# The first gated layer by Strassen's scheme, with the code of the last layer, and x fetched in parts

## The chip, the cores and the metric

The kernel runs on one core of one Trainium2 chip. The metric is the time of one execution on the device in microseconds (us); the median of three runs counts. The engines are TensorE (matmuls), VectorE, ScalarE, GpSimd and SyncE (which only issues DMAs here). In the profile they are called PE, DVE, ACT, POOL and SP; PEld is TensorE's loading of weights.

## The reference

625 tokens of width 1024 in float32. A graph layer comes first (`x + gnn(layernorm(x))`), then a feed-forward block on the layer-normalised rows:

```python
h = x @ lin0_w + lin0_b
h = _swiglu(h, swi1_w1, swi1_b1, swi1_w2, swi1_b2)   # silu(x @ w1 + b1) * (x @ w2 + b2), the first gated layer
h = _moe(h, ...)                                      # top 4 of 8 experts, plus a shared expert
h = h @ lin1_w + lin1_b
h = _swiglu(h, swi2_w1, swi2_b1, swi2_w2, swi2_b2)   # the last layer
```

The result is added to x. All weights are 1024 x 1024, save those of the gate (8 x 1024) and the shared expert (twice as wide).

## The kernel before

Activations are kept transposed: eight chunks of 128 features by 628 columns (625 tokens, padded to two halves of 314, the second with 312 real columns). Precision is kept by splitting each operand in a high and a low part of type fp32r, and by three matmuls per chunk: high x high, weights high x activations low, weights low x activations high (`products`, line 1672). A **unit** is the weights of 128 outputs, [128, 8 chunks, 128]; it is 3 x 8 matmuls for each half of the tokens, 48 in all. Units come from a stream in DRAM: SyncE loads them to four buffers `raw` (line 407 on), ScalarE rounds them to `w_hi` (`split_hi`, 475), GpSimd subtracts to `w_lo` (`split_lo`, 479). All order is written out by hand, with semaphores; each engine works its own program in order.

**lin0** (eight units, line 1878 on) writes `b_hi` and `b_lo`: ScalarE adds the bias (`linear_hi`, 761), VectorE takes the low part (`linear_lo`, 1154). **swi1**, the first gated layer, is 16 units, gate and up in turn (`gated`, 1864): ScalarE takes SiLU of the gate's bank (`gated_pair`, 768), VectorE multiplies (`gated_pair`, 1161), both split the product into `a_hi`, `a_lo`, TensorE turns it to rows (`h_turn`, 1895), and VectorE copies them to `rows` (`h_rows`, 1183). From there they are stored for the gathers of the experts. Then follow the first half of the shared expert (**sha**), eight experts, the other half (**shb**), **lin1** and **swi2**.

**swi2**, the last layer, runs by Strassen's scheme in Winograd's form. Activations and weights are cut in quarters, and seven products of quarters replace eight. A **set** q (0 to 7) is the seven products that give 128 near and 128 far outputs of gate (even q) or up (odd q); a product t is 4 chunks x 3 = 12 matmuls (`quad_product`, 2118). The seven are named by the quarter of the activations, `A11, S2, S3, S1, A12, A22, S4`; set 0 takes them in the order `FIRST_ORDER` (0, 4, 6, 1, 2, 3, 5). Sums of weight quarters are VectorE's: S1, S3, S2 in `sums_first` (1480), S4 in `sum_last` (1489). ScalarE makes each high part (`quad_high`, 869), VectorE each low part (`quad_low`, 1498), save four of set 0, which are GpSimd's (`POOL_QUADS`, 622). VectorE also puts the products together: with u2 (1577), u3 (1583), C22 and u4 (1590, 1591), and the additions of `add_in_place` (1555); ScalarE copies the first product to `p1` (926) and takes SiLU of four quarters (`gate_quad`, 916). TensorE starts set 1 when the second SiLU of set 0 is there, and its product A22 (t = 5) when u3 is. In lin1 the outputs are computed in the order `LIN1_ORDER`, and VectorE forms the sums of activation quarters (`t_sums`, 1504) on the way. Raw weights of set q can be loaded when set q - 2 has been split. The x to be added at the end is fetched in one DMA of 2.5 MB (905), issued as set 0 starts.

Of the kernel before, what the change touches and what calls it, by code (L numbers as in the profile page):

```python
# [10 lines left out]
P = 128  # L11
# [36 lines left out]
def build(nc, x, src, dst, gnn_b, biases, gate, stream, out):  # L48
# [16 lines left out]
    with ctx:  # L65
# [75 lines left out]
        gate_both = act_x[:, 0, 0:KC * GW].rearrange("p (k n) -> p k n", n=GW)  # L141
# [50 lines left out]
        POOL_QUADS = (0, 4, 6, 5)  # L192
        DVE_QUADS = (1, 2, 3)
# [10 lines left out]
        t4_tmp = yr[:, 0:HK * HT].rearrange("p (k n) -> p k n", n=HT)  # L204
        p1, u2 = [yr[:, (HK + n) * HT:(HK + n + 1) * HT] for n in range(2)]
        u4_u3 = yr[:, (HK + 2) * HT:(HK + 4) * HT].rearrange("p (s n) -> p s n", n=HT)
# [10 lines left out]

        def quad_source(q, t):
# [79 lines left out]
        lin0 = Stage("lin0", U_LIN0, gates=False)  # L298
# [4 lines left out]
        lin1_lo = sem("lin1_lo")  # L303
        swi2 = Stage("swi2", U_SWI2, parts=False)
        sha_y = sem("sha_y")
# [93 lines left out]
        LAST_STORES = ((7, 3, NT, 7), (8, 0, 2, 3), (9, 0, 3, 7), (10, 2, NT, 3))  # L399
        out_tiles = out.rearrange("(i p) d -> p i d", p=TT)  # L400
# [6 lines left out]
        def _(sp):  # L407
# [18 lines left out]
            with sp.Fori(1, U_EXP // RING) as g:  # L426
                load_four(g * RING, g * RING)
# [7 lines left out]
            for j, m in enumerate(LIN1_ORDER):  # L435
                sp.wait_ge(hi_split, U_LIN1 + j + 1 - RING)
                sp.wait_ge(lo_split, U_LIN1 + j + 1 - RING)
                sp.dma_start(raw[:, j % RING, :], stream[U_LIN1 + m, :, :]).then_inc(raw_loaded[j % RING], 16)
            for p in range(HK):
                for s, u in enumerate((2 * p, 2 * (p + HK), 2 * p + 1, 2 * (p + HK) + 1)):  # L440
                    q = 2 * p + s // 2
                    if p == 0:
                        sp.wait_ge(hi_split, U_SWI2 - RING + s + 1)
                        sp.wait_ge(lo_split, U_SWI2 - RING + s + 1)
                    elif s % 2 == 0:
                        last_raw = max(RAW_QUADS, key=lambda t: quad_place(q - 2, t))
                        sp.wait_ge(quad_hi, quads_until(q - 2, last_raw))
                        if q == 2:
                            sp.wait_ge(pool_quad_lo, len(POOL_QUADS))
                        else:  # L450
                            sp.wait_ge(dve_quad_lo, lows_until(q - 2, 5))
                        sp.wait_ge(s_sum, 4 * (q - 2) + 4)
                    sp.dma_start(raw[:, s, :], stream[U_SWI2 + u, :, :]).then_inc(raw_loaded[s], 16)
# [6 lines left out]
        def pair_loaded(eng, q):  # L460
            for s in range(2):
                eng.wait_ge(raw_loaded[2 * (q % 2) + s], 16 * (U_SWI2 // RING + q // 2 + 1))

        def arrived(eng, u, off):
            s = off % RING
            if isinstance(u, int):
                eng.wait_ge(raw_loaded[s], 16 * ((u + off) // RING + 1))
                if u + off >= RING:
                    eng.wait_ge(unit_done, u + off - RING + 1)
# [5 lines left out]
        def split_hi(u, off):  # L475
            s = arrived(nc.scalar, u, off)
            nc.scalar.activation(w_hi[:, s, :], raw[:, s, :], ACT.Copy).then_inc(hi_split, 1)  # L477

        def split_lo(u, off):
# [9 lines left out]
            last.then_inc(lo_split, 1)  # L489
# [3 lines left out]
        def _(pool):  # L493
# [36 lines left out]
            for u in range(U_LIN0, U_SHA):  # L530
                split_lo(u // RING * RING, u % RING + 3)
# [89 lines left out]
            pair_loaded(pool, 0)  # L621
            for t in POOL_QUADS:
                n = quad_place(0, t)
                pool.wait_ge(quad_hi, n + 1)
                for c in (slice(0, HW // 2), slice(HW // 2, HW)):
                    last = pool.tensor_tensor(wlo8[:, n, c], quad_source(0, t)[:, c],
                                              whi8[:, n, c].bitcast(f32), ALU.subtract)
                last.then_inc(pool_quad_lo, 1)
# [3 lines left out]
        def _(act):  # L632
# [128 lines left out]
            def linear_hi(st, o_hi, b, pairs):  # L761
                for m in range(KC):
                    split_hi(st.base, m + 3)
                    act.wait_ge(unit_done, st.base + m + 1)
                    act.activation(halves(o_hi[:, m, :]), acc_dense(pairs[m]), ACT.Identity,
                                   bias=bias[:, b, m:m + 1]).then_inc(st.hi, 1)

# [14 lines left out]
            linear_hi(lin0, b_hi, B_LIN0, LIN0_PAIRS)  # L782
            act.wait_ge(gate_loaded, 16)
            act.activation(gate_both[:, :, 0:EXPERTS], gate_cols, ACT.Copy).then_inc(gate_split, 1)
            for m in range(KC):
                gated_pair(swi1, m, a_hi, B_S1A)
# [82 lines left out]
            def quad_high(q, t):  # L869
                n = quad_place(q, t)  # L870
                if n >= 8:
                    act.wait_ge(quad_done, n - 7)
                else:
                    act.wait_ge(unit_done, U_SWI2 - RING + n // 2 + 1)
# [1356 lines left out]
```

## Time and profile before

| | |
|---|---|
| median of three runs | 1587.01 us (1586.23 to 1588.19) |
| the profiled execution's own time | 1587.09 us |
| its span, first to last instruction | 1585.4 us |
| TensorE busy | 1567.0 us (99%), 10892 matmuls |
| VectorE, ScalarE, GpSimd busy | 570.5, 549.0, 799.2 us |
| lin0, from 176.40 | 48.80 us |
| swi1, 225.20 to 341.72 | 116.52 us |
| swi2, from 1470.92 to the end of the span | 114.5 us |

A row of a timeline gives start, duration, engine, line, operation, what it writes and reads, and in brackets how long the engine had stood idle before it and who released it. A matmul's duration includes its latency; two that follow each other overlap, so their distance, not their duration, is their cost.

### The profile page before, as it was taken

How to read it: one execution, taken by the hardware profiler on the slowest of the kernel's cores; microseconds unless marked ns; L12 is line 12 of the kernel's file. 1: busy time of each engine (PE TensorE's matmuls, PEld its weight loads, DVE VectorE, ACT ScalarE, POOL GpSimd, SP SyncE). 2: the span in 40 equal slices, each digit the busy share in tenths (PEclk: the TensorE clock that was granted, in tenths of full speed). 3: DMA queues.
4: the chain of work that ended last, by engine and by line, in shares of the span. 5: the costliest groups of instructions: out<-in, count | busy, mean ns of one | idle time of the engine just before them, and what ended most of it. 6: DMA issues, size and time to landing. Idle time of an engine off the chain costs nothing.

```text
span 1585.4 us, 28313 instructions
## 1 busy us (share of the span) xinstructions
PE 1567.0 (99%) x10892; PEld 1549.6 (98%) x10892; DVE 570.5 (36%) x1045; ACT 549.0 (35%) x824; POOL 799.2 (50%) x673
## 2 busy tenths in 40 slices
PE   9999999999999999999999999999999999999898
PEld 8998999999999999999999999999999999999898
DVE  8665311113420113224241322424221156125787
ACT  6332222222222333343434344344444322224442
POOL 1311233333433666768677686868777576333000
PEclk9999999999999999999999999999999999999999
DMA  4412222232232445546464554646555486221422
GB/s 134 132 41 76 83 67 80 67 108 95 82 98 80 144 142 168 169 126 216 134 191 159 180 170 152 202 143 205 159 175 166 135 221 195 69 78 54 121 88 82
DMA packets 66590, 205.64 MB, mean 130 GB/s; under 512 B 13585, under 2 KB 17335, under 8 KB 66480
## 3 DMA queue, kind: packets, MB, share of 16 engines
q1 hardware_dynamic: 45020, 157.94, 32.8%
q0 software_dynamic: 14976, 32.81, 6.6%
q10 hardware_dynamic: 6484, 13.26, 2.5%
q8 instruction: 88, 1.44, 0.4%
q14 instruction: 22, 0.18, 0.0%
HBM read 185.01 MB, written 18.95 MB: 129 GB/s over the span
## 4 chain that ended last, share of the span: by engine, by line
PE 95%; DVE 2%; ACT 1%; POOL 1%; issue 1%; DMA 0%; SPq 0%; ACTq 0%; POOLq 0%; DVEq 0%
PE acc L1676 88%; PE acc L1656 2%; PE acc L1976 1%; PE acc L1955 1%; POOL w_lo L487 1%; PE acc L1725 0%; DVE yrow L975 0%; ACT act_b L640 0%; DMA rows<-x_dram 0%; DVE yrow L976 0%; POOL gath L539 0%; PE acc L1912 0%; PE acc L2029 0%; PE acc L1667 0%; ACT act_b L645 0%
## 5 line engine op out<-in xcount | busy, mean ns | idle before, releaser
L487 POOL TENSOR_TENSOR w_lo<-raw,w_hi 128x512 fp32r<-128x512 f32 x560 | 718.2, 1308 | 594.0 <-ACT w_hi L477 571.8
L1676 PE MATMUL acc<-act_b,w_hi 128*128 128x314 f32 (+8 forms) x2304 | 512.6, 311 | 0.5 <-ACT gath L918 0.5
L1676 PE MATMUL acc<-act_x,w_hi 128*128 128x344 f32 (+8 forms) x2176 | 479.9, 309 | 4.0 <-POOL w_lo L487 2.6
L1676 PE MATMUL acc<-act_a,w_hi 128*128 128x312 f32 (+1 forms) x1856 | 408.4, 309 | 4.3 <-DVE yrow L1583 4.3
L1676 PEld LDWEIGHTS acc<-act_b,w_hi 128*128 128x128 f32 x2304 | 383.7, 189 | 1.1 <-issue 1.1
L1676 PEld LDWEIGHTS acc<-act_x,w_hi 128*128 128x128 f32 x2176 | 363.7, 188 | 6.0 <-issue 4.8
L1676 PE MATMUL acc<-act_b,w_lo 128*128 128x314 f32 (+8 forms) x1152 | 355.1, 308 | 0.0
L1676 PE MATMUL acc<-act_x,w_lo 128*128 128x312 f32 (+8 forms) x1088 | 336.0, 309 | 0.0
L1676 PEld LDWEIGHTS acc<-act_a,w_hi 128*128 128x128 f32 x1856 | 309.2, 190 | 4.9 <-issue 3.0
L477 ACT ACTIVATE w_hi<-raw 128x1024 fp32r<-128x1024 f32 x280 | 293.8, 1050 | 5.4 <-DVE rows L1189 2.8
L1676 PE MATMUL acc<-act_a,w_lo 128*128 128x312 f32 (+1 forms) x928 | 285.2, 307 | 0.0
L1676 PEld LDWEIGHTS acc<-act_b,w_lo 128*128 128x128 f32 x1152 | 217.6, 189 | 0.0
L1676 PEld LDWEIGHTS acc<-act_x,w_lo 128*128 128x128 f32 x1088 | 204.6, 188 | 0.0
L1676 PEld LDWEIGHTS acc<-act_a,w_lo 128*128 128x128 f32 x928 | 175.4, 189 | 0.0
L1347 DVE TENSOR_TENSOR prod<-acc,silu 128x344 f32<-128x344 f32 x64 | 33.0, 516 | 293.5 <-PE acc L1676 293.5
L1350 DVE TENSOR_TENSOR act_b<-prod,act_b 128x344 fp32r<-128x344 f32 x64 | 98.8, 1543 | 35.7 <-ACT act_b L817 34.0
L817 ACT ACTIVATE act_b<-prod 128x344 fp32r<-128x344 f32 x64 | 31.5, 492 | 188.3 <-DVE prod L1347 177.0
L1339 DVE COPY yrow<-acc 128x256 f32<-128x256 f32 x64 | 27.1, 424 | 172.1 <-PE acc L1976 172.1
L823 ACT ACTIVATE prod<-acc 128x344 f32<-128x344 f32 x64 | 29.3, 457 | 133.4 <-PE acc L1676 133.4
L1329 DVE TENSOR_TENSOR act_x<-acc,act_x 128x344 fp32r<-128x344 f32 x64 | 33.1, 517 | 80.3 <-ACT act_x L797 80.3
L814 ACT ACTIVATE silu<-acc 128x344 f32<-128x344 f32 x64 | 29.2, 456 | 92.9 <-PE acc L1676 92.9
L1656 PE MATMUL acc<-yrow 125*125 125x314 bf16 (+1 forms) x400 | 55.6, 297 | 2.4 <-DVE yrow L976 2.4
(238 smaller groups left out, 1022.8 us busy)
## 6 DMA issues: line engine op xcount, KB each, us to landing
raw<-stream_dram SPq DMA_DIRECT2D x296, 512.0 KB
y_dram<-yrow POOLq DMA_DIRECT2D x16, 512.0 KB
rows<-x_dram ACTq DMA_DIRECT2D x2, 2500.0 KB
y_dram<-yrow POOLq DMA_DIRECT2D x8, 352.0 KB
x_dram<-rows ACTq DMA_DIRECT2D x5, 500.0 KB
h_rows_dram<-rows ACTq DMA_DIRECT2D x1, 2500.0 KB
rows<-x_dram SPq DMA_DIRECT2D x5, 448.0 KB
out_dram<-rows ACTq DMA_DIRECT2D x2, 560.0 KB
```

The lines of the kernel that those rows point to most:

```text
L477: nc.scalar.activation(w_hi[:, s, :], raw[:, s, :], ACT.Copy).then_inc(hi_split, 1)
L487: last = nc.gpsimd.tensor_tensor(w_lo[:, s, c], raw[:, s, c], w_hi[:, s, c].bitcast(f32), ALU.subtract)
L814: act.activation(silu[:, 0:CAP], acc[:, 2 * m % 4, 0:CAP], ACT.Silu).then_inc(exp.silu, 1)
L817: act.activation(g_hi[:, m, :], prod[:, m % 2, 0:CAP], ACT.Copy).then_inc(exp.hi, 1)
L823: act.activation(prod[:, m % 2, 0:CAP], acc[:, m % 4, 0:CAP], ACT.Copy).then_inc(yt_copied, 1)
L1329: dve.tensor_tensor(e_lo[:, m, :], acc[:, TPB + 2 + m % 2, 0:CAP], e_hi[:, m, :].bitcast(f32), ALU.subtract).then_inc(xe_lo, 1)
L1339: dve.tensor_copy(yrow[:, 0:2, m * P:(m + 1) * P], b[:, 0:2 * P].rearrange("p (s d) -> p s d", d=P))
L1347: dve.tensor_tensor(prod[:, m % 2, 0:CAP], acc[:, (2 * m + 1) % 4, 0:CAP], silu[:, 0:CAP], ALU.mult).then_inc(exp.prod, 1)
L1350: dve.tensor_tensor(g_lo[:, m, :], prod[:, m % 2, 0:CAP], g_hi[:, m, :].bitcast(f32), ALU.subtract).then_inc(exp.lo, 1)
L1656: last = pe.matmul(outs[i], oh_dst[0:TT, s, i * TT:i * TT + rows_of(i)], oh_src[0:TT, s, :], start=False, stop=ends)
L1676: ins = pe.matmul(o, w, xs_[h], start=(first and w is hi and xs_ is x_hi), stop=(last and w is lo))
L1955: last = pe.transpose(acc[:, TPB + 2 + m % 2, c0:c0 + cn], grow[0:cn, n, m * P:(m + 1) * P], ident[0:cn, 0:cn])
```

## The change

swi1 takes the scheme of the last layer, and the code of both becomes one. The class `Seven` holds the offsets of the semaphores' counts; `linear_high`, `linear_low`, `quads`, `quad_sums`, `seven` and `load_seven` are the former code of lin1 and swi2 with a parameter `L`. lin0's units come in the order `LIN1_ORDER`.

For swi1, ScalarE and VectorE split the four quarters of outputs as pairs (`out_high`, `out_low`), TensorE turns them (`h_turn`), and ScalarE copies the rows (`h_rows`) that VectorE copied before. Its A22 activations lie in chunks 3 and 7 of `a_hi` and `a_lo`. The first unit of sha is run as two half units, its chunks in the order 0, 4, 1, 5, 2, 6, 7, 3, each waiting for its own output, with the last two turns behind the halves.

For both layers: the low part of the A22 weights of set 0 goes from GpSimd to VectorE; `sums_first` of set 1 stands behind u2 of set 0; `low(1, 0)` behind u3, and so on, as the diff shows; `u4_u3` moves from `yrow` to `gath`. In the last layer x is fetched in four parts of two blocks of 128 columns each (0.64 MB), one at the old place and one after each of the sets 1, 3 and 5.

```diff
-        LIN0_PAIRS = (0, 1, 3, 2, 0, 1, 3, 2)
+        LIN0_PAIRS = (0, 1, 3, 2, 0, 1, 0, 1)
-        POOL_QUADS = (0, 4, 6, 5)
-        DVE_QUADS = (1, 2, 3)
+        POOL_QUADS = (0, 4, 6)
+        DVE_QUADS = (1, 2, 3, 5)
...
+            def raw_free(self, eng, q):
+                last_raw = max(RAW_QUADS, key=lambda t: quad_place(q, t))
+                eng.wait_ge(quad_hi, self.quads + quads_until(q, last_raw))
+                if q == 0:
+                    eng.wait_ge(pool_quad_lo, self.pool_lows + len(POOL_QUADS))
+                eng.wait_ge(dve_quad_lo, self.dve_lows + lows_until(q, 5))
+                eng.wait_ge(s_sum, self.quad_sums + 4 * q + 4)
...
-            act.dma_start(rows[0:TT, :, :], x1_dram.rearrange("(i p) d -> p i d", p=TT)).then_inc(x1_back, 16)
+            def fetch_x1(p):
+                if p >= 1:
+                    act.wait_ge(x1_back, 32 * p)
+                for m in (p, p + HK):
+                    act.dma_start(rows[0:TT, :, m * P:(m + 1) * P], x1_tiles[:, :, m * P:(m + 1) * P]
+                                  ).then_inc(x1_back, 16)
+            fetch_x1(0)
+            def fetch_next(q):
+                if q % 2 == 1 and q + 1 < KC:
+                    fetch_x1(q // 2 + 1)
...
+            def out_high(p, side):
+                m = p + HK * (1 - side)
+                act.wait_ge(swi1.prod, 4 * p + 3 + side)
+                if p == HK - 1:
+                    act.wait_ge(quad_done, quads_until(KC - 1, 5))
+                act.activation(a_hi[:, m, 0:HT + HL], prod[:, 1 - side, 0:HT + HL], ACT.Copy).then_inc(swi1.hi, 1)
+            def h_rows(p, side):
+                m = p + HK * (1 - side)
+                act.wait_ge(h_tp, 2 * p + side + 1)
+                act.activation(rows[0:TT, 0:4, m * P:(m + 1) * P],
+                               acc[0:TT, TPB, :].rearrange("p (i d) -> p i d", d=P), ACT.Copy)
+                act.activation(rows[0:TT, 4, m * P:(m + 1) * P], acc[0:TT, TPB + 1, 0:P],
+                               ACT.Copy).then_inc(h_copied, 1)
+            linear_high(TWO[0])
+            quads(TWO[0], pair_high, far_rows, near_rows)
...
             # VectorE, one set of either layer (quad_sums)
+                    if more and q >= 1:
+                        sums_first(L, q + 1)
+                        quad_low(L, q + 1, 0)
+                    dve.wait_ge(p1_saved, L.p1 + q + 1)
+                    dve.wait_ge(quad_done, L.quads + quads_until(q, 1))
+                    dve.tensor_tensor(u2, acc[:, 1, 0:HT], p1, ALU.add).then_inc(u_done, 1)
+                    if q == 0:
+                        sums_first(L, 1)
+                    elif more:
+                        quad_low(L, q + 1, 1)
+                        sum_last(L, q + 1)
...
+                    dve.tensor_tensor(u4_u3[:, 1, :], acc[:, 3, 0:HT], u2, ALU.add).then_inc(u_done, 1)
+                    if is_gate and p >= 1:
+                        take_out(p - 1, 0)
+                    if q == 0:
+                        quad_low(L, 1, 0)
+                    elif more:
+                        quad_low(L, q + 1, 2)
...
+                    if q == 0:
+                        quad_low(L, 1, 1)
+                        sum_last(L, 1)
+                        quad_low(L, 1, 2)
+                    if more:
+                        quad_low(L, q + 1, 3)
...
             # TensorE
+            seven(TWO[0], h_turn, {})
+            pe.wait_ge(swi1.prod, 4 * (HK - 1) + 2)
+            half_unit(U_SHA, 0, a_hi, a_lo, 0, 0, out_ready, LIN1_ORDER[:6] + (7, 3))
+            h_turn(HK - 1, 0)
+            half_unit(U_SHA, 0, a_hi, a_lo, 1, 1).then_inc(unit_done, 1)
+            h_turn(HK - 1, 1)
```

## Rows read from the trace of the kernel before

**Rows 1.** The page, parts 1 and 2: busy time and share; granted clock in tenths.

```profile
PE 1567.0 (99%) x10892; PEld 1549.6 (98%) x10892; DVE 570.5 (36%) x1045; ACT 549.0 (35%) x824; POOL 799.2 (50%) x673
...
PEclk9999999999999999999999999999999999999999
```

**Rows 2.** The page, part 4: the chain that ended last, by engine.

```profile
PE 95%; DVE 2%; ACT 1%; POOL 1%; issue 1%; DMA 0%; SPq 0%; ACTq 0%; POOLq 0%; DVEq 0%
```

**Rows 3.** Stretch swi1: length; busy PE, PEld, DVE, ACT, POOL; clock; DMA share, GB/s.

```profile
225.20:341.72 116.52, 116.10 (x810) 115.91 (x810) 18.54 (x30) 29.49 (x35) 40.62 (x32) 1.00 0.24 74
```

**Rows 4.** Chain of waits within swi1: start, duration, what.

```profile
253.09 0.55 PE acc L1725 x5
...
268.13 13.91 PE acc L1676 x96
...
339.98 0.88 DVE prod L1170
```

**Rows 5.** Stretches of swi2: sets 2 and 3; sets 4 and 5.

```profile
1507.01:1532.49 25.48, 25.48 (x181) 25.48 (x180) 22.53 (x43) 10.62 (x20) 0.00 (x0) 1.00 0.25 87
1532.49:1557.96 25.47, 25.47 (x180) 25.47 (x180) 22.50 (x43) 10.51 (x20) 0.00 (x0) 1.00 0.34 116
```

**Rows 6.** Timeline of PE in the first sets of swi2.

```profile
1470.92 0.46 PE L1676 MATMUL acc<-act_b,w_hi 128*128 128x314 f32 x2
...
1484.88 0.53 PE L1676 MATMUL acc<-act_a,w_hi 128*128 128x314 f32 x2 [2.82 <-DVE yrow L1583]
...
1487.71 0.86 PE L1676 MATMUL acc<-act_b,w_hi 128*128 128x314 f32 x2 [0.53 <-ACT gath L918]
...
1499.25 0.53 PE L1676 MATMUL acc<-act_a,w_hi 128*128 128x314 f32 x2 [1.52 <-DVE yrow L1583]
...
1502.81 0.46 PE L1676 MATMUL acc<-act_b,w_hi 128*128 128x314 f32 x2
```

**Rows 7.** A split of an output on DVE (timeline); the last product (chain).

```profile
341.65 0.81 DVE L1175 TENSOR_TENSOR act_a<-prod,act_a 128x628 fp32r<-128x628 f32 x1 [0.79 <-ACT act_a L780]
...
1580.73 0.56 DVE prod L1569
```

**Rows 8.** Timeline of DVE in sets 0 and 1 of swi2.

```profile
1479.08 1.24 DVE L1484 TENSOR_TENSOR acc<-raw 128x512 f32<-128x512 f32 x1
...
1481.97 0.68 DVE L1501 TENSOR_TENSOR w_lo<-raw,w_hi 128x512 fp32r<-128x512 f32 x1
1482.57 0.47 DVE L1577 TENSOR_TENSOR yrow<-acc,yrow 128x314 f32<-128x314 f32 x1
1482.96 0.68 DVE L1501 TENSOR_TENSOR w_lo<-acc,w_hi 128x512 fp32r<-128x512 f32 x1
...
1486.53 0.48 DVE L1557 TENSOR_TENSOR acc<-acc,yrow 128x314 f32<-128x314 f32 x1
...
1494.63 0.70 DVE L1484 TENSOR_TENSOR acc<-raw 128x512 f32<-128x512 f32 x1 [4.62 <-DMA raw<-stream_dram]
```

**Rows 9.** Timeline of ACT: the second SiLU of set 0 of swi2.

```profile
1487.04 0.52 ACT L918 ACTIVATE gath<-acc,bias 128x314 f32<-128x314 f32 x1 [0.86 <-DVE acc L1557]
```

**Rows 10.** Timeline of POOL in set 0 of swi2.

```profile
1478.25 2.65 POOL L626 TENSOR_TENSOR w_lo<-raw,w_hi 128x256 fp32r<-128x256 f32 x2 [17.11 <-ACT w_hi L879]
```

**Rows 11.** Stretch with the lower clock, columns as in rows 3.

```profile
1486.25:1489.75 3.50, 2.97 (x13) 2.61 (x12) 3.22 (x7) 2.71 (x6) 0.00 (x0) 0.51 0.45 137
```

**Rows 12.** Timeline of ACT before the first SiLU of swi1.

```profile
227.13 1.28 ACT L775 ACT_TABLE_LOAD   x1
```

**Rows 13.** Timeline of ACT: a copy from PSUM of 500 columns.

```profile
176.01 0.59 ACT L736 ACTIVATE act_a<-acc 128x500 fp32r<-128x500 f32 x1 [5.17 <-PE acc L1835]
```

**Rows 14.** The issue of x (timeline of ACT), and a stretch behind it.

```profile
1475.54 0.49 ACTq L905 DMA_DIRECT2D rows<-x_dram  x1
...
1480.00:1488.00 8.00, 4.65 (x28) 4.06 (x27) 7.72 (x15) 3.08 (x7) 0.90 (x1) 0.90 0.71 187
```

**Rows 15.** Timeline of ACT in set 5 of swi2: four issues of result rows.

```profile
1552.23 2.86 ACTq L909 DMA_DIRECT2D out_dram<-rows  x4
```

More of the change, by code:

```diff
@@ L434, in _ @@
                 load_four(g * RING, g * RING)
[L435 to L453, printed above, removed]
+            load_seven(TWO[1])
             for count, i0, i1, m in LAST_STORES:
@@ L620, in _ @@
                 split_lo(u // RING * RING, u % RING + 3)
[L621 to L628, printed above, removed]
+            quad_lows(TWO[1])
         @block.scalar
@@ new lines, in pair_high, with far_rows, near_rows @@
+            def pair_high(q):
+                if q >= 2 and q % 2 == 0:
+                    out_high(q // 2 - 1, 0)
+                    out_high(q // 2 - 1, 1)
+            def far_rows(q):
+                if q >= 2 and q % 2 == 0:
+                    h_rows(q // 2 - 1, 0)
+            def near_rows(q):
+                if q >= 2 and q % 2 == 0:
+                    h_rows(q // 2 - 1, 1)
+                if q == KC - 1:
+                    for u in range(3):
+                        split_hi(U_SHA, u)
+                    for side in range(2):
+                        out_high(HK - 1, side)
@@ L1678, in products, with unit @@
                 return ins
-            def unit(u, off, x_hi, x_lo, banks, width, ready=None):
+            def unit(u, off, x_hi, x_lo, banks, width, ready=None, count=1):
                 s = off % RING
@@ L1696, in unit, with half_unit @@
                                         w_lo[:, s, k * P:(k + 1) * P], xx[0], xx[1], k == 0, k == KC - 1)
-                last.then_inc(unit_done, 1)
-            def half_unit(u, off, x_hi, x_lo, bank, h, between=None):
+                last.then_inc(unit_done, count)
+            def half_unit(u, off, x_hi, x_lo, bank, h, between=None, order=range(KC)):
                 s = off % RING
@@ L1704, in half_unit @@
                 pe.wait_ge(lo_split, u + off + 1)
-                for k in range(KC):
+                for k in order:
                     if between is not None:
@@ L1864, in gated, with seven @@
+            def seven(L, turn, last_between):
+                for q in range(KC):
+                    for n in range(NQ):
+                        t = FIRST_ORDER[n] if q == 0 else n
+                        quad_product(L, q, t, last_between.get(t) if q == KC - 1 else None)
+                        if q >= 2 and q % 2 == 0 and t in (1, 4):
+                            turn(q // 2 - 1, t // 4)
             def gated(st, x_hi, x_lo, first_ready, after=None, freed=None, begun=False):
@@ L2176, in near_tiles @@
                     last_turn(1, TPB + 3, 0, 3)
[L2178 to L2183 removed]
+            seven(TWO[1], o_turn, {5: far_tiles, 6: near_tiles})
             pe.wait_ge(swi2.prod, 4 * 3 + 4)
```

665 lines of the change are left out of this document (349 added, 316 removed).

## The prediction

> **What bounds the kernel now.** I read the page's parts 1 and 2 first: TensorE is busy 99% of the span, at full clock in all forty slices [rows 1]. Then part 4: 95% of the chain that ended last is TensorE [rows 2]. So time goes only where matmuls go, or where a wait of TensorE appears or vanishes. Next the stretches of the two gated layers. In the first (225.20 to 341.72) TensorE works 116.10 of 116.52 us, while VectorE, ScalarE and GpSimd have 18.5, 29.5 and 40.6 us of work [rows 3]. In its chain 96 matmuls take 13.91 us, 0.145 us each, a turn of rows 0.55, and only at the end something else stands, the last product on VectorE [rows 4]. Last the layer that already runs by seven products, since the changed layer takes its code. Its steady part is clean: 25.5 us for two sets of seven, TensorE busy throughout, VectorE 22.5, ScalarE 10.6 [rows 5]. Its first two sets are not: set 0 starts at 1470.92, TensorE has waits that end at 1484.88, 1487.71 (where set 1 starts) and 1499.25, and set 2 starts at 1502.81 [rows 6]. That is 31.89 us for 2 x 84 matmuls that need 24.4: 7.5 us lost.
>
> **Part 1, matmuls.** Removed: 16 units of 48 = 768. Added: 8 sets x 7 products x 4 chunks x 3 = 672. 96 fewer, 13.9 us off the engine that bounds [rows 4]. The eight turns stay (4.4 us), and the two half units that open the next layer are the 48 matmuls of the unit they replace.
>
> **Part 2, the end of the first layer.** Before, 116.52 less 768 x 0.145 and 4.4 leaves 0.7 us, the wait for the last product. After, the next layer starts at once and takes the two last outputs only in its chunks 7 and 3. From the last quarter product VectorE adds (0.48), multiplies (0.56) and splits two outputs (0.81 each) [rows 7, 8]: 2.7 us; TensorE has 21 matmuls = 3.0 us before it needs the second. Hidden, so I take 0.7 off; bounds 0 and 0.7.
>
> **Part 3, set 0 of the first layer.** This stall is new there, and I size it by following VectorE's queue in the last layer. Before, it ran from 1479.08 without a gap: S1, S3, S2, low(1,0), u2, low(1,1), S4, u3, low(1,2), C22, u4, low(1,3), then at 1486.53 the addition that releases the SiLU at 1487.04, which releases set 1 [rows 8, 9]. (low(q,t) is the low part of weights of product t in set q; u and C are sums of products.) After, the queue reads: low(0,5) (taken over from GpSimd), u2, S1, S3, S2, u3, low(1,0), C22, u4, low(1,1), S4, low(1,2), low(1,3), the same addition. Successive starts give 0.60 for an operation of 512 columns and 0.39 for one of 314. S1, S3 and S2 took 2.89 together, not 1.80, with GpSimd at work from 1478.25 to 1480.90; S1 alone took 1.24 there and 0.70 at 1494.63, with GpSimd idle [rows 8, 10]. GpSimd has left its last piece to VectorE, so I use 0.60. Sum: 9 x 0.60 + 4 x 0.39 = 6.96, where it was 7.45. Set 1 starts 0.5 us earlier, 16.3 us after set 0 instead of 16.8. u3 ends some 2.3 us earlier, which shortens the wait at 1484.88, but what is late next is the SiLU, so this time comes back as a wait of about 2.9 us before set 1. Stall of set 0 in either layer: 16.3 - 12.2 = 4.1 us; the first layer has the same queue and takes it whole. Bounds: 3.7 (its data come 0.4 earlier, as the linear layer's last unit is no longer pressed by anything) and 5.2 (S1 and S3 slow again).
>
> The clock belongs to this. From 1486.25 to 1489.75 it was granted at 0.51, the lower of its two levels, 1.2 GHz instead of 2.4, after TensorE had stood for 2.8 us and run again for 1.4; of 2.97 us of matmuls half was lost, 1.46 [rows 6, 11]. The new stall is of the same kind and I take 1.3 us in each layer; bounds 0 and 1.7. The Trainium skill (TensorE: Matmul & The Clock Gate, What's actually happening) says that the monitor is free-running and does not start with the kernel; by that the same stall may be caught or missed, and the sum would be this one or 2.6 us less. One fall in one trace can't decide it.
>
> ScalarE meets one thing here that the last layer lacks: its first SiLU loads a table, 1.28 us [rows 12]. Behind its splits of S2, S3 and S1 (about 1483.5 on the last layer's clock) it would end at 1484.8; the first SiLU is then done at 1485.3, and the one that matters can start at 1486.6. Cost 0, with 1.3 us of cover. The Trainium skill (ScalarE: Activation LUTs, What ACT_TABLE_LOAD costs) adds a drain of about 1380 ns to the load; by that the estimate is a cost of 0.1 us. The row can't show it, since ScalarE had nothing to do behind the load.
>
> **Part 4, sets 1 to 7 of the first layer.** The work of the last layer, except that on VectorE two splits of outputs (0.81) stand for the sums of result rows, and ScalarE gets two output splits (0.7) and two copies of rows (0.59 for 500 columns and some 0.3 for the rest) on top: 10.6 + 3.2 = 13.8 us in 25.5 [rows 5, 7, 13]. Cost 0: in the steady part neither engine held TensorE up. If that cover is gone, about 1 us per even set, 3 us.
>
> First layer: -13.9 - 0.7 + 4.1 + 1.3 = **-9.2 us**.
>
> **Part 5, the last layer.** Its set 0 gains 0.5. In set 1 VectorE stood 4.62 us for the weights of set 2, until 1494.63, and was so late with u3 that TensorE waited until 1499.25 [rows 6, 8]. This 1 MB could be issued when GpSimd finished at 1480.9 and shared the engines with the 2.5 MB of x issued at 1475.54; 187 GB/s moved [rows 14]. After, the first part of x has 0.64 MB. At the same 187 GB/s from 1476 on, 1.7 MB are there by 1485; VectorE asks for them at 1489.1 (the addition, two more, three splits). Then u3 of set 1 is ready by 1494 and TensorE wants it at 1497: the wait goes, 1.7 us with its restart, and nothing is late next. The clock's loss stays (1.3 for 1.5). Before 7.5 lost, after 4.1 + 1.3 = 5.4: **-2.1 us**; bounds 0 and -3.5. The later parts are issued by ScalarE between sets. Four issues of this kind took its queue 2.86 us at 1552.23, and TensorE ran on [rows 5, 15]. Two cost half; in set 5 six together end about 1.4 us later, and the copy behind them is due when u2 is, some 1.5 us after its data. Cost 0; uncovered 0.7 per part, 2 us.
>
> Moved scratch space, shared counters, the gate's columns and the other bank pairs of the linear layer cost nothing: bank pair 0 is asked for again a unit (7 us) after ScalarE could read it, and its two reads take 1.6. On SyncE's queue the same loads stand in the same order; those of set 2 wait for VectorE's low(0,5) at 1479.7, not for GpSimd's at 1480.9.
>
> **Sum.** -9.2 - 2.1 = -11.3 us. The profiled execution took 1587.09 (its span 1585.40), the median of the runs is 1587.01, 0.1 lower: forecast **1575.8 us**.
>
> **Rivals.**
> *Clock not caught*: neither stall brings it down. For: the waits are 0.5 us shorter in sum. Against: the longest one stays as long [rows 6, 11]. 1575.8 - 2.6 = 1573.2. Chance 0.12.
> *ScalarE's added work is late*: the output splits stand ahead of the quarter splits in its order. Against: it is busy 54% of the set. 1575.8 + 3 = 1578.8. Chance 0.10.
> *The parts come too slowly*: pieces of 512 bytes instead of 4 KB hold the weights up all the same, and the 1.7 us of set 1 don't go. For: each part has as many pieces as the whole. Against: 4 us of slack. 1577.5. Chance 0.08.
> *Slower*: GpSimd's reads. While it works an operation of VectorE with two SBUF inputs takes 0.54 us more [rows 8, 10]. VectorE has 11.3 us of work in a set of 12.7 and becomes the bound once GpSimd meets more than two of its eight such operations in a set. All eight: 4.3 more, 2.9 over, over seven sets 20 us, so 1596. Against: GpSimd's program has nothing to do between set 0 and the end of set 7, where VectorE has little left. Chance 0.03.
> Forecast 0.67.
>
> **How the numbers follow.** The first three rivals and the bounds of parts 3 and 5 give 1573.0 to 1579.5; the slower one lies outside. What a measurement can tell from no change is about 0.2%, 3.2 us, so everything below 1583.8 is faster. Faster 0.95, same 0.02 (several losses at once), slower 0.03.
>
> **What would show it.** 96 matmuls fewer. In the first layer 106 us from the start of set 0 to the next layer's first matmul, with two turns behind it. In each gated layer one wait of about 2.9 us before set 1, and one of 0.7 before the product on A22; full clock from set 2 on; in the last layer no wait of VectorE for weights in set 1. Wrong if TensorE waits in sets 2 to 7 of the first layer, if the linear layer before it grows, or if the experts' stretch changes.

## The result, and the profile after

The changed kernel took 1579.13 us (median of five runs, 1576.38 to 1581.06) where the kernel before took 1587.01 (1586.23 to 1588.93): ratio 0.9946, 95% interval 0.9935 to 0.9956. (The ratios of this document are not quotients of the two medians beside them; by the ratio the gain is 8.6 us.) So it is faster by 7.9 us; forecast were 11.2, and the time lies inside the range of 1573.0 to 1579.5, near its slow end. The profiled execution took 1576.51 us (span 1574.8), 10.6 less than that of before: the forecast's 11.3 nearly holds there. That is in part luck: in this execution the clock did not fall in the last layer, and this hid about as much as a wait that the forecast did not have.

The page after: busy time, granted clock, and the chain by engine. 96 matmuls fewer and 12.7 us less of TensorE's time than in [rows 1]; more of the chain is off TensorE than the 5% of [rows 2].

```profile
PE 1554.3 (99%) x10796; PEld 1536.2 (98%) x10796; DVE 658.4 (42%) x1207; ACT 584.2 (37%) x913; POOL 764.6 (49%) x645
...
PEclk9999999999999999999999999999999999999999
...
PE 93%; DVE 3%; POOL 1%; issue 1%; ACT 1%; ACTq 0%; DVEq 0%; POOLq 0%
```

The stretch of the first gated layer, two of its steady sets, set 1 of the last layer and two steady sets there (columns as in [rows 3]):

```profile
225.22:331.56 106.34, 102.81 (x704) 102.13 (x703) 86.99 (x157) 54.95 (x102) 7.05 (x6) 0.98 0.27 89
276.93:302.40 25.47, 25.47 (x181) 25.47 (x180) 22.40 (x41) 13.16 (x26) 0.00 (x0) 1.00 0.24 83
1478.65:1494.40 15.75, 15.75 (x109) 15.75 (x110) 13.59 (x26) 7.70 (x15) 0.00 (x0) 1.00 0.29 90
1507.00:1532.48 25.48, 25.48 (x180) 25.48 (x180) 22.51 (x43) 10.64 (x21) 0.00 (x0) 1.00 0.34 108
```

The first layer takes 106.3 us from set 0 to the next layer's first matmul (forecast 106), and its steady sets are the last layer's: 25.47 us with ScalarE at 13.2 (forecast 13.8). All that it loses is in its first 20 us. TensorE's timeline, set 0 and the start of set 1 of that layer (the bracket is the wait before the row, and who ended it):

```profile
232.19 0.52 PE L1773 MATMUL acc<-act_x,w_hi 128*128 128x314 f32 x2 [0.29 <-DVE act_b L1291]
...
236.89 0.52 PE L1773 MATMUL acc<-act_a,w_hi 128*128 128x314 f32 x2 [0.58 <-DVE gath L1351]
...
241.52 0.53 PE L1773 MATMUL acc<-act_b,w_hi 128*128 128x314 f32 x2 [2.66 <-ACT gath L849]
241.89 0.36 PE L1773 MATMUL acc<-act_b,w_lo 128*128 128x314 f32 x1
242.04 0.73 PE L1773 MATMUL acc<-act_b,w_hi 128*128 128x314 f32 x2
...
245.59 0.30 PE L1773 MATMUL acc<-act_x,w_lo 128*128 128x314 f32 x1
```

Set 0 starts at 225.22 and set 1 at 241.52: 16.3 us, as forecast, with the long wait where it was forecast. From 242.0 to about 245.5 a matmul takes 0.46 to 0.47 instead of 0.31. The stretch within it (columns as in [rows 3]), and the chain over set 1:

```profile
242.00:245.20 3.20, 3.20 (x15) 3.20 (x14) 3.07 (x6) 2.71 (x6) 0.00 (x0) 0.50 0.31 61
```

```profile
240.85 0.53 ACT gath L849
241.38 0.14 issue
241.52 17.40 PE acc L1773 x108
258.92 0.55 PE acc L1822 x5
```

108 matmuls at 0.145 need 15.7 and took 17.4 in this chain; TensorE's timeline has the turn at 258.76, 17.2 us after the start of set 1. The lower level (1.2 GHz) cost 1.5 us by the timeline. ScalarE ahead of it, with the table load of the first layer:

```profile
237.98 1.28 ACT L849 ACT_TABLE_LOAD   x1
239.27 0.52 ACT L849 ACTIVATE gath<-acc,bias 128x312 f32<-128x312 f32 x1
240.85 0.52 ACT L849 ACTIVATE gath<-acc,bias 128x314 f32<-128x314 f32 x1 [1.06 <-DVE acc L1322]
```

The load was hidden: behind it ScalarE still had 1.06 us to wait for the addition. The last layer, TensorE's timeline:

```profile
1469.32 0.52 PE L1773 MATMUL acc<-act_x,w_hi 128*128 128x314 f32 x2 [0.29 <-DVE act_b L1291]
...
1474.02 0.53 PE L1773 MATMUL acc<-act_a,w_hi 128*128 128x314 f32 x2 [0.58 <-DVE gath L1351]
...
1478.65 0.53 PE L1773 MATMUL acc<-act_b,w_hi 128*128 128x314 f32 x2 [2.65 <-ACT gath L849]
...
1552.31 0.78 PE L1822 MATMUL acc<-ident,prod 128*125 128x128 f32 x5 [1.04 <-DVE rows L1711]
```

The wait of 1.52 us in set 1 [rows 6] is gone, and in this execution the clock stayed up. But at 1552.31, in set 6, there is a wait that the kernel before didn't have. The chain that leads to it goes back to ScalarE's queue (ACTq are the instructions on it that issue DMAs), here as its timeline at the end of set 5, and the stores' first two pieces in the chain:

```profile
1540.31 0.63 ACT L816 ACTIVATE w_hi<-gath 128x512 fp32r<-128x512 f32 x1 [1.11 <-PE acc L1773]
1540.32 1.79 ACTq L1007 DMA_DIRECT2D rows<-x_dram  x2
1542.15 5.75 ACTq L1014 DMA_DIRECT2D out_dram<-rows  x4
1548.03 0.63 ACT L816 ACTIVATE w_hi<-raw 128x512 fp32r<-128x512 f32 x1 [7.08 <-PE acc L1773]
```

```profile
1542.15 2.96 ACTq L1014
...
1545.14 1.64 ACTq L1014
```

Issuing six DMAs held ScalarE for 7.6 us; the four stores alone had taken 2.86 [rows 15], and behind the part of x the same four take 5.75, most of it the first two. (The last row's bracket names PE, but in the chain the issues stand right before that split.) ScalarE's next split is late, so VectorE's low part and sums are, and among them the addition to `rows` that frees the bank of the next turn.

### The profile page after: what moved, and what is told of

Read it like the earlier page. It is cut to its first block, busy times and chain, and to the rows that moved or that the text cites. A ratio compares the mean times of both kernels' runs of the same rounds, so it can differ in the third digit from the quotient of the medians.

```text
span 1574.8 us, 28380 instructions
## 1 busy us (share of the span) xinstructions
PE 1554.3 (99%) x10796; PEld 1536.2 (98%) x10796; DVE 658.4 (42%) x1207; ACT 584.2 (37%) x913; POOL 764.6 (49%) x645
## 4 chain that ended last, share of the span: by engine, by line
PE 93%; DVE 3%; POOL 1%; issue 1%; ACT 1%; ACTq 0%; DVEq 0%; POOLq 0%
PE acc L1773 86%; PE acc L1753 2%; PE acc L2144 1%; PE acc L2123 1%; POOL w_lo L512 1%; DVE yrow L1056 1%; DVE yrow L1055 1%; PE acc L1822 0%; ACTq L1014 0%; DVE w_lo L1278 0%; POOL gath L577 0%; PE acc L2080 0%; PE acc L2197 0%; PE acc L1738 0%; PE acc L1764 0%
## 5 line engine op out<-in xcount | busy, mean ns | idle before, releaser
L512 POOL TENSOR_TENSOR w_lo<-raw,w_hi 128x512 fp32r<-128x512 f32 x528 | 680.9, 1316 | 609.8 <-ACT w_hi L502 587.6
L1773 PE MATMUL acc<-act_x,w_hi 128*128 128x312 f32 (+8 forms) x2304 | 508.5, 309 | 4.3 <-POOL w_lo L512 2.6
L1773 PE MATMUL acc<-act_b,w_hi 128*128 128x312 f32 (+8 forms) x2048 | 456.9, 312 | 5.3 <-ACT gath L849 5.3
L1773 PE MATMUL acc<-act_a,w_hi 128*128 128x314 f32 (+1 forms) x1920 | 422.6, 309 | 1.2 <-DVE gath L1351 1.2
L1773 PEld LDWEIGHTS acc<-act_x,w_hi 128*128 128x128 f32 x2304 | 385.6, 188 | 6.6 <-issue 4.8
L1773 PE MATMUL acc<-act_x,w_lo 128*128 128x312 f32 (+8 forms) x1152 | 355.8, 309 | 0.0
L1773 PEld LDWEIGHTS acc<-act_b,w_hi 128*128 128x128 f32 x2048 | 340.9, 189 | 5.8 <-issue 5.8
L1773 PE MATMUL acc<-act_b,w_lo 128*128 128x314 f32 (+8 forms) x1024 | 316.0, 309 | 0.0
L1773 PE MATMUL acc<-act_a,w_lo 128*128 128x314 f32 (+1 forms) x960 | 294.8, 307 | 0.0
L1773 PEld LDWEIGHTS acc<-act_b,w_lo 128*128 128x128 f32 x1024 | 193.5, 189 | 0.0
## 6 DMA issues: line engine op xcount, KB each, us to landing
rows<-x_dram ACTq DMA_DIRECT2D x8, 312.5 KB
```

The lines of the kernel that those rows point to most:

```text
L512: last = nc.gpsimd.tensor_tensor(w_lo[:, s, c], raw[:, s, c], w_hi[:, s, c].bitcast(f32), ALU.subtract)
L1773: ins = pe.matmul(o, w, xs_[h], start=(first and w is hi and xs_ is x_hi), stop=(last and w is lo))
```

## Stages of the executions

Each ratio is against runs of the kernel before on the same chip (medians 1587.0, 1588.5, 1587.7 and 1587.4 in the four series), and the text goes by it rather than by the difference of medians. "Start" is when TensorE begins its last turn of rows ahead of lin0, "middle" from there to the end of the 0.3 us wait in set 0 of the last layer (7 us into it), then "sets 0, 1" from there to the first turn (early in set 2), and "sets 2 to 7" from that to the end of the last wait of TensorE; each is a difference of starts in TensorE's timeline of the one profiled execution.

| kernel | median us | ratio to before, 95% | start | middle | sets 0, 1 | sets 2 to 7 |
|---|---|---|---|---|---|---|
| before | 1587.01 | 1 | 175.38 | 1302.52 | 28.41 | 75.02 |
| changed | 1579.13 | 0.9946 (0.9935 to 0.9956) | 175.57 | 1293.75 | 25.08 | 76.31 |
| changed, again | 1579.34 | 0.9943 (0.9930 to 0.9956) | 177.67 | 1293.76 | 26.58 | 76.29 |
| x whole | 1576.52 | 0.9928 (0.9915 to 0.9941) | 175.57 | 1293.55 | 27.79 | 75.03 |
| parts, stores by SyncE | 1576.71 | 0.9925 (0.9911 to 0.9938) | 177.58 | 1292.91 | 25.07 | 75.02 |
| last layer alone | 1588.45 | 0.9999 (0.9990 to 1.0007) | 177.60 | 1303.64 | 25.07 | 77.33 |
| last layer, order alone | 1586.40 | 0.9998 (0.9989 to 1.0007) | 176.00 | 1302.97 | 25.63 | 75.52 |
| last layer, parts alone | 1588.50 | 1.0007 (0.9997 to 1.0017) | 174.94 | 1302.67 | 25.56 | 77.47 |
| early addition | 1571.83 | 0.9900 (0.9884 to 0.9917) | 177.54 | 1290.84 | 23.00 | 76.23 |
| free bank | 1571.97 | 0.9903 (0.9886 to 0.9919) | 175.06 | 1290.63 | 23.54 | 76.38 |
| both | 1571.87 | 0.9905 (0.9888 to 0.9921) | 175.39 | 1289.53 | 23.00 | 76.68 |
| both, x whole | 1574.74 | 0.9924 (0.9910 to 0.9937) | 175.85 | 1292.19 | 27.18 | 75.02 |
| all edits | 1570.54 | 0.9897 (0.9881 to 0.9914) | 175.06 | 1290.78 | 23.01 | 75.03 |

## Experiments

**The changed kernel again**, for a second profile. Two theories on what the median lacks stood against each other: A, ScalarE's issues block it for a time that varies; B, the clock behind the stall of the last layer.

> The changed kernel once more, beside the kernels of this call. Theory A (ScalarE's DMA issues in the last layer block it for a time that varies): the profile again shows the four stores at the end of set 5 as a block of 5 us or more and TensorE waiting about 1 us in set 6, and where the block is longer the wait and the whole time are longer. Theory B (the clock after the stall of set 0 of the last layer): the profile has the same block, but a time near 1578 to 1580 goes with a granted clock near 0.5 for 3 us behind that stall, and one near 1576.5 with a clock of 1.00 there. Both: ratio to the kernel before 0.9935 to 0.9956, as it was.

The stores took 5.53 us and the wait was again 1.04, so in these two profiles A's cost is steady: it costs, but nothing shows that it spreads the runs. The clock did fall in the last layer this time (TensorE's stretch from 1481, columns busy, matmuls, clock, DMA):

```profile
1481.00:1485.00 4.00, 4.00 (x20) 0.64 0.36 88
```

Sets 0 and 1 took 26.58 for 25.08: 1.5 us. Another 2.1 us were lost before anything of the change runs, in "start"; that is treated in the last section.

**x fetched whole, at the old place.**

```diff
-            fetch_x1(0)
+            act.dma_start(rows[0:TT, :, :], x1_tiles).then_inc(x1_back, 16)
...
-                if q % 2 == 1 and q + 1 < KC:
-                    fetch_x1(q // 2 + 1)
```

> x fetched as one DMA at the old place, the rest as in the changed kernel. Theory A: with no fetch of a part at the end of set 5 the stores on ScalarE's queue take about 2.9 us again in place of 7.5, TensorE's wait of 1.0 us in set 6 is gone, and the spread of the runs is again near 2.7 us. Against it stands what the one DMA costs in set 1: if the weights of set 1 come late again, TensorE waits up to 1.5 us there. Sum between 1.0 us faster and 0.5 us slower than the changed kernel (median 1578.1 to 1579.6). Theory B: median as the changed kernel's within 0.5 us but for that wait, and the spread stays at 4 to 5 us. The rival of the forecast that the order of VectorE's work alone removed the weights' wait: no wait in set 1.

The block shrank and the wait in set 6 went, 76.3 to 75.03 us. ScalarE at the end of set 5:

```profile
1542.83 2.95 ACTq L1007 DMA_DIRECT2D out_dram<-rows  x4
```

The median is 2.8 us lower than the changed kernel's beside it. That is more than the 1.3 the trace shows and more than was expected; the intervals overlap. The one transfer did hold up the weights, by 2.85 us for VectorE, and TensorE did not wait, but it ran at the lower level itself for about 6 us (2.7 us lost) and so needed the products later. VectorE in set 1, and TensorE's stretch from 1481:

```profile
1483.59 0.70 DVE L1252 TENSOR_TENSOR acc<-raw 128x512 f32<-128x512 f32 x1 [2.85 <-DMA raw<-stream_dram]
```

```profile
1481.00:1485.00 4.00, 4.00 (x18) 0.56 0.97 250
```

The spread of the runs stayed at 4.9 us, which is against A. It is not proof of B: the 17 runs of the kernel before in this series spread over 5.2 us, where five had spread over 2.7 at first.

**Parts and stores issued by SyncE.**

```diff
                         sp.dma_start(raw[:, s, :], stream[L.swi + u, :, :]).then_inc(raw_loaded[s], 16)
+                    if L.n == 1:
+                        fetch_x1(p)
...
             load_seven(TWO[1])
+            sp.wait_ge(o_rows, 4)
+            store(0, NT, 0, 2 * P)
+            store(0, NT, HK * P, (HK + 2) * P)
```

> The parts of x and the output stores of sets 5 and 7 issued by SyncE, none by ScalarE in the sets of the last layer. Theory A: no block on ScalarE, no wait of TensorE in set 6, 1.0 us off the profiled time and the spread back near 2.7 us; median about 1577.5. Theory B: the 1.0 us goes too, but the spread of 4 to 5 us stays, since the clock is what varies. A loss of 1 us or more in sets 2 to 7 would show that the loads on SyncE's queue, which now stand behind parts and their waits, are late.

No block, sets 2 to 7 back at 75.02, weights in time, 1576.71. The spread was 6.1 us. So the parts cost nothing by themselves, and neither do the stores on ScalarE's queue (75.03 with x whole); what costs is both on ScalarE's queue. Parts by SyncE with the stores left to ScalarE were not run.

**Only the last layer's share, and its two halves.** The kernel before with the last layer's order and parts; with the order alone; with the parts alone.

```diff
-POOL_QUADS = (0, 4, 6, 5)
-DVE_QUADS = (1, 2, 3)
+POOL_QUADS = (0, 4, 6)
+DVE_QUADS = (1, 2, 3, 5)
...
+            fetch_x1(0)
...
+                if q % 2 == 1 and q + 1 < KC:
+                    fetch_x1(q // 2 + 1)
```

> The kernel before with the last layer's new order and the parts of x, its first layer left with eight products. Forecast's sum: 2.1 us faster than the kernel before (ratio 0.9987), so the first layer is worth 9.2. By the trace of the changed kernel: the last layer there gave 3.6 with the clock kept, or 2.1 with it lost, less 1.0 for the new wait in set 6, so 1.1 to 2.6 us faster (ratio 0.9984 to 0.9993). Theory A: its spread is wide, like the changed kernel's. Theory B: also wide, if the clock of the last layer is what varies; a narrow spread would put the variation in the first layer, where the stall of set 0 is new.

> The kernel before with only the new order of the last layer (A22's low part on VectorE, the sums and low parts of set 1 moved), x still fetched as one DMA. My prediction took 0.5 us from set 0 and 1.7 from the weights of set 1. If the order alone brings the weights in time (they are free earlier, since SyncE's wait is met sooner), the wait of 1.5 us in set 1 is gone and from the start of set 0 to the first turn is 32.1 us as in the changed kernel with the clock kept, 2.1 to 3.3 us less than before: ratio 0.998 to 0.9985. If the parts of x are needed for it, the wait in set 1 stays at 1 us or more, and VectorE waits for the weights' DMA until some 21 us after the start of set 0. In both, ScalarE's four stores at the end of set 5 take 2.9 us, and no wait of TensorE in set 6.

> The kernel before with x fetched in parts and nothing else of the change. If the parts make the weights of set 1 come in time, the wait of 1.5 us in set 1 goes; set 0 stays as it was, with its waits of 2.8 and 0.5 us. Against it ScalarE's queue: the part and the four stores at the end of set 5 hold ScalarE 7 to 9 us, and TensorE waits 1.0 to 1.9 us in set 6 and the set before, as measured in the kernel with the last layer's change alone. Sum: -1.7 + 1.3 to 2.3, so within 0.6 us of the kernel before on either side: same.

The last layer's change is worth nothing that can be measured: 0.9999, where 0.9987 was forecast. The first layer's is the difference, 0.9999 - 0.9943 = 0.0056 of 1588.5, 8.9 us (forecast 9.2), give or take 2.4 by the two intervals. The stretches agree: 116.52 less 106.34, less the two turns of 0.55 that now stand behind the next layer's start, is 9.1. Where the 2.1 us went, the trace says: sets 0 and 1 gained 3.3, of which 1.3 is the clock (kept in this execution, lost in that of before) and 2.0 the order and the parts, and sets 2 to 7 gave 2.3 back, 1.85 of it in two waits in set 6. TensorE's timeline of the kernel with the last layer's change alone:

```profile
1562.08 0.53 PE L1697 MATMUL acc<-act_b,w_hi 128*128 128x314 f32 x2 [0.65 <-ACT yrow L934]
...
1565.26 0.78 PE L1746 MATMUL acc<-ident,prod 128*125 128x128 f32 x5 [1.20 <-DVE rows L1557]
```

The halves: with the order alone VectorE's wait for the weights fell from 4.62 to 2.32 us and TensorE's from 1.52 to 0.31, between the two outcomes expected:

```profile
1492.92 0.70 DVE L1483 TENSOR_TENSOR acc<-raw 128x512 f32<-128x512 f32 x1 [2.32 <-DMA raw<-stream_dram]
```

```profile
1497.55 0.53 PE L1684 MATMUL acc<-act_a,w_hi 128*128 128x314 f32 x2 [0.31 <-DVE yrow L1585]
```

With the parts alone both are gone, but sets 2 to 7 take 77.47. So either half removes most of the wait that the forecast counted once for both. By their intervals neither half can be told from no change. In this kernel VectorE got the weights 4.62 us after the start of set 1 with the clock kept; with x whole in the changed kernel it was 5.15 us, so at full clock TensorE would have waited some 0.8 us there (an estimate from these rows).

**The stall before set 1.** What else is to be had there? TensorE waits 2.65 us for the SiLU of C11, and that for an addition standing behind four operations of VectorE whose results are due later. First edit:

```diff
                     if q == 0:
+                        add_in_place(4, p1, HT)
                         quad_low(L, 1, 1)
...
-                    add_in_place(0 if q else 4, p1, HT)
+                    if q >= 1:
+                        add_in_place(0, p1, HT)
```

> The changed kernel with the addition for C11 of set 0 moved ahead of the low part of A22, of S4 and of two more low parts on VectorE, in both gated layers. Theory (the stall of 2.65 us before set 1 is VectorE's order, since SiLU of C11 waits for the addition behind four other operations): in the last layer the addition starts 2.4 us earlier, the wait before set 1 falls from 2.65 us to 0.1 to 0.5, and TensorE's clock stays at 1.00 behind it; in the first layer ScalarE loads its table (1.28 us) ahead of the first SiLU, so the wait there falls only to about 1.3. Sum: 2.3 and 1.3 us of waits, and 1.2 to 1.5 us of clock in the first layer if it is kept: 3.5 to 5 us under the changed kernel, near 1575. Rival (the low parts behind it become late, since set 1 needs them in its first 3 us): a wait of 0.5 us or more before A22's or S4's product of set 1, and under 2 us gained.

The wait fell to 0.24 us in the last layer and 1.49 in the first, where the table load now stands in the way. TensorE's timeline, and ScalarE's and VectorE's ahead of the first of these waits:

```profile
242.32 0.53 PE L1775 MATMUL acc<-act_b,w_hi 128*128 128x314 f32 x2 [1.49 <-DVE w_lo L1278]
...
1475.30 0.53 PE L1775 MATMUL acc<-act_b,w_hi 128*128 128x314 f32 x2 [0.24 <-DVE w_lo L1278]
```

```profile
239.95 1.28 ACT L849 ACT_TABLE_LOAD   x1
241.24 0.93 ACT L849 ACTIVATE gath<-acc,bias 128x312 f32<-128x312 f32 x2
```

```profile
241.50 0.68 DVE L1278 TENSOR_TENSOR w_lo<-gath,w_hi 128x512 fp32r<-128x512 f32 x1
```

The bracket names VectorE's low part, which ended at 242.18. That one is low(1,2), and the first product of set 1 doesn't wait for it; what the code makes it wait for is the second of the two SiLUs, which ended at 242.17.

From 242.32 to the turn it takes 15.71 us: the clock was kept. The median is 1571.83, ratio 0.9900 for 0.9943, 6.8 us by the ratios; 3.5 to 5 were expected. The traces show 2.7 of it in the first layer and 2.1 (against the changed kernel with the clock kept) to 3.6 (lost) in the last. The rest fits the clock as recorded for every run, not only the profiled one: its mean over the execution was 0.996 to 0.998 in the five runs of the changed kernel beside the first experiments, 0.9972 on average, and 1.000 in all four here. 0.0028 of 1575 us is 4.4 us of matmul time, an estimate from figures rounded to 0.001; with the 3.6 us of shorter waits that is 8.0, for 6.8 by the ratios and 7.5 by the medians.

Second edit. In set 0 C11 has a bank of its own, so bank 0 is free once product 0 is copied out; TensorE's wait for two SiLUs there names a bank that it doesn't write.

```diff
-                if t == 0:
+                if t == 0 and q == 1:
+                    pe.wait_ge(p1_saved, L.p1 + 1)
+                elif t == 0:
...
+                elif t == 3 and q == 1:
+                    pe.wait_ge(u_done, L.u + 3)
```

> The changed kernel with one wait less for a reason: in set 0 the sum C11 stands in a bank of its own, so the first product of set 1 waits for the copy of product 0 out of bank 0 instead of the SiLU of C11; the order of the other engines is as it was. Theory (the stall is only a wait for a bank that is free anyway): the wait of 2.65 us before set 1 is gone in both layers, and a shorter one comes later in set 1, where the third product needs bank 3, whose SiLU ends 2 us behind that of C11: product 2 is due 3.1 us into set 1, so a wait of about 1.2 us. Gain 1.4 us per layer, and since neither wait is above 1.3 us the clock is kept: 1.2 to 1.5 us more per layer where it fell. Sum 3 to 5.5 us under the changed kernel. Rival (the total idle time decides the clock, not the longest wait): gain of 2.5 to 3 only.

As expected, 2.65 became a later wait of 1.1 in either layer (1571.97, ratio 0.9903, 6.4 us by the ratios where 3 to 5.5 were expected):

```profile
242.98 0.54 PE L1773 MATMUL acc<-act_b,w_hi 128*128 128x314 f32 x2 [1.14 <-ACT gath L849]
...
1476.98 0.52 PE L1773 MATMUL acc<-act_b,w_hi 128*128 128x314 f32 x2 [1.10 <-ACT gath L849]
```

and the clock was 1.00 behind both. In the first layer, set 0 lost the clock in all four profiles with the 2.65 us wait in one piece and keeps it here with waits of 0.3, 0.6 and 1.1. That does not decide against the rival by which the sum of idle time counts, since that sum also fell, from 3.5 to 2.0; that both longest wait and sum are smaller is all that is shown. Both edits together:

> Both edits, the early addition and the free bank. Theory: no wait over 0.3 us before or in set 1 of the last layer; in the first layer the table load of 1.28 us still stands before the SiLUs, and it now delays only the third product, by up to 1 us. Sum against the changed kernel: 2.65 + 2.65 of waits less 0.3 and 1.0, so 4.0, and the clock of 1.3 to 2.7 us where it fell: near 1573.5 to 1575. If the clock still falls in the first layer with waits this short, the idle time of set 0 (0.29 and 0.58) is what it reacts to, and the sum is 4 us.

0.3, 0.6 and 0.4 us of waits are left in either layer, and sets 0 and 1 take 23.00. The median (1571.87) is no lower than with one edit, so of what the second edit adds the runs can show nothing. The traces have a little: from the 0.3 us wait of the first layer to its turn 22.99 us, against 23.86 with the early addition alone and 23.53 with the free bank alone, and in the last layer 23.00 against 23.00 and 23.54. That is 0.9 to 1.1 us in all, less than the spread of these runs (3.0 us).

**Both edits, x whole.** This takes away the stall behind which one transfer looked harmless.

> The changed kernel with the early addition and the free bank, and x fetched as one DMA at the old place. With x whole the weights of set 1 landed 2.9 us after VectorE asked for them, and TensorE did not wait, but its clock was low there for 6 us and it was late by 2.7 us. Here set 0 has no stall and the clock should be kept, so the cover is gone: if the parts are worth something, TensorE waits 1 to 2.5 us in set 1 of the last layer for a product whose low part is late, and the sum is -1.2 (no block in set 6) + 1 to 2.5 against the kernel with both edits and the parts by ScalarE (1571.9): 1571.7 to 1573. If one transfer does no harm after all: 1570.5 to 1571, as with SyncE's issue.

TensorE waited 2.81 us in set 1 and lost the clock on top: sets 0 and 1 took 27.18, 4.2 us more than 23.00. TensorE, VectorE and ScalarE in set 1:

```profile
1484.66 0.86 PE L1764 MATMUL acc<-act_b,w_hi 128*128 128x314 f32 x2 [2.81 <-ACT yrow L862]
```

```profile
1483.54 0.70 DVE L1252 TENSOR_TENSOR acc<-raw 128x512 f32<-128x512 f32 x1 [4.29 <-DMA raw<-stream_dram]
```

```profile
1483.57 0.63 ACT L816 ACTIVATE w_hi<-raw 128x512 fp32r<-128x512 f32 x1 [5.14 <-DMA raw<-stream_dram]
1484.10 0.41 ACT L862 ACTIVATE yrow<-acc 128x314 f32<-128x314 f32 x1
```

The way it came was not the expected one, a late low part of VectorE's. What TensorE waited for is ScalarE's copy of the first product (`yrow`, L862), and in ScalarE's program that copy stands behind the split of the next set's raw weights, which waited 5.14 us for the DMA. An order in which the copy comes first was not run.

The median is 1574.74 for 1571.87, more than forecast; the two were measured on different chips, and their ratios, 0.9924 and 0.9905, have intervals that overlap. The traces show it more plainly: 4.2 us lost in sets 0 and 1, 1.7 gained in sets 2 to 7. So the parts are worth about 2.5 us once set 0 is quick, with the stores' queue left as it is.

**All edits**: both, the parts and stores by SyncE, and the SiLU table loaded ahead of the layer, by this line of ScalarE's before lin0:

```diff
+            act.activation(ones[0:TT, 1:2], ones[0:TT, 0:1], ACT.Silu)
```

> Both edits, the SiLU table loaded ahead of the layer by a SiLU of one element a row, and the parts of x and the stores of sets 5 and 7 issued by SyncE. Theory: besides the gains of the two edits, the wait of 1.0 us in set 6 is gone (1.2 us as measured between the changed kernel and the one with SyncE's issue) and 1 us at the table load. Median 1571 to 1573; against the kernel before a ratio near 0.990. Rival: the kernel's opening, 0 or 2.1 us later in all kernels so far, and the clock elsewhere hide part of it: the median above 1573.

1570.54 us, ratio 0.9897: 7 to 9 us below the changed kernel (by ratios or by medians), a little under its expected range. Sets 0 and 1 at 23.01 and sets 2 to 7 at 75.03 are the best seen in one kernel; over the kernels with one edit its lead of 1.3 us is within the intervals. The earlier table load gave nothing here: from the 0.3 us wait of the first layer to its turn it takes 23.01 us with it and 22.99 without, since with the free bank no SiLU holds TensorE.

## Why the prediction was right, and where it was not

*Matmuls (-13.9) and the end of the layer (-0.7)*: 96 fewer; the next layer begins at 331.56 without a wait. *Set 0 (+4.1)*: 16.30 us in the first layer, 16.31 in the last, for 16.3. Following VectorE's queue by successive starts was exact (from low(0,5) at 233.37 to the addition at 240.33, 6.96 for 6.96), and the prediction that u3's earlier end comes back as a wait before set 1 too (2.65; forecast 2.9). *Table, splits and copies (0)*: hidden.

*Clock (+1.3 in each layer)*: right in kind, near in size for the first layer, and no constant in the last. In the first layer TensorE's timeline has from the start of set 1 to the first turn 17.24, 16.99, 17.27 and 16.97 us in the four profiles that have the stall, for 15.71 without: 1.3 to 1.6 lost each time. In the last layer the same span took 15.75, 17.25, 18.47, 15.75 and 15.74 in five profiles: nothing, 1.5, 2.7, nothing, nothing (a sixth, with the order alone, 15.99 without its wait of 0.31); 2.7 lies beyond the bound of 1.7. The old order of set 0 shows the same: with waits of 2.8 us and 0.5 to 0.8 before set 1 the kernel before lost 1.3 us, and the one with the parts alone nothing (15.75). The rule weighed in part 3 (the Trainium skill, TensorE: Matmul & The Clock Gate, What's actually happening: a free-running monitor) fits the last layer, where one stall of 2.65 us was caught in some executions and missed in others, but in the first layer it was caught every time. Why the two layers differ no run shows.

*First layer*: 8.9 us measured by difference and 9.1 by the stretches, 9.2 forecast.

*Last layer (-2.1)*: 0.2 us measured, between 1.6 gained and 1.1 lost. The step that failed is part 5's "in set 5 six together end about 1.4 us later" and its "Cost 0". Six issues held ScalarE 7.6 us, not 4.3; the sets after it took 1.3 us longer in the changed kernel and 2.3 longer with the last layer alone. I had one row (four stores, 2.86 us) and assumed that issues add up. Four stores cost 2.9 alone and 5.5 to 6.9 right behind a part's two issues. The forecast named the uncovered cost itself (0.7 per part, 2 us) and gave it no rival. With 1.3 us put there it is 1577.1, and with the clock as measured in the four profiles with the stall (from 1.3 less to 1.7 more) 1575.8 to 1578.8, for a median of 1579.1. What is left is smaller than what "start" alone varies by, 2.1 us. (The sum is off by 0.1: 1587.0 - 11.3 is 1575.7.)

*Rivals*: ScalarE's added work in the first layer was not late (TensorE has no wait there behind set 1); the parts did not come too slowly. GpSimd had no occasion to slow VectorE: it has no operation from 215.4 to 322.9, VectorE's nine wide operations of set 0 ran at 0.60 us each, and beside GpSimd's six in set 7 TensorE did not wait. "Clock not caught" happened, for one of the two layers, in the profiled execution.

What stays open: the 2.8 us between the changed kernel and x whole are more than the 1.3 that the traces show. The recorded clocks suggest chance for a part: 0.9972 on average in the changed kernel's runs beside it and 0.9978 with x whole, about 1 us. And the "middle" varies by up to 2.7 us among kernels with the same work there (1289.53 and 1292.19 with both edits); with one or two profiles of a kernel that can't be laid to an edit.

## What to carry to other kernels

A wait of the bounding engine costs its length and, where the clock falls behind it, more: here 1.3 to 1.6 us on 2.65 in the first layer. Breaking this wait into smaller ones, or moving one addition, in both layers, was worth 6 to 7 us here, beside the 8 to 9 of the whole change. Ask of each wait whether the releaser is the one needed (the bank written next, not a count that happens to cover it), and of each in-order queue whether the operation that releases someone stands behind ones that release nobody yet. Don't put several DMA issues in a row on an engine that feeds the bounding one when another queue is idle, and don't size several issues as a sum of single ones.

## What the runs showed of the hardware

- An issue on ScalarE's queue holds ScalarE itself. Two issues of a part of x (rows of 512 bytes, 312.5 KB each) took 1.2 to 2.5 us, four stores 2.9, the same stores behind such a part 5.4 to 6.9. What in the queue makes them wait was not tested.
- The kernel's opening comes at several speeds, whichever kernel it is: "start" is 174.9 to 176.0 us in nine profiles and 177.5 to 177.7 in four. TensorE's matmuls run at about half the rate until about 5, 7 or 11 us, with a granted clock of 1.00 in the record all along. The same stretch of the changed kernel's first profile and of its second (length, busy TensorE and matmuls, clock, DMA share, GB/s):

```profile
8.00:10.00 2.00, 2.00 (x17) 1.00 1.06 258
```

```profile
8.00:10.00 2.00, 2.00 (x9) 1.00 1.04 254
```

This alone makes 2.1 us between two executions, a quarter of what was to be measured.
- The table load is followed at once by the next operation (237.98 + 1.28, then 239.27), and it follows at once on the one before, which ended at 237.96: of the drain that the Trainium skill adds to it (ScalarE: Activation LUTs, What ACT_TABLE_LOAD costs) these rows show nothing.
